# Expert bias, key and value weights and the last late tile moved across the border of two blocks

## The reference

```
x = x + attention0(LN(x), ctx, ctx)      # 64x64 products over the sequence axis, 8 heads, softmax
x = x + experts(LN(x))                   # logits x @ W_gate + b_gate, top 2 of 8 experts,
                                         # mean of relu(x @ W_e + b_e) over the two
x = x + attention1(LN(x), ctx, ctx)      # 32 query heads, 8 key/value heads of 16: k = ctx @ Wk, v = ctx @ Wv
x = x + ffn(LN(x))                       # silu(gate) * up, 1376 wide, then down
```

## Time and profile before

| | us |
|---|---|
| median of 3 runs | 899.8 (897.63 to 900.2) |
| the profiled execution | 902.44 |
| its span, first to last instruction | 900.7 |
| PE busy | 851.1 (94%) |
| DVE, ACT, POOL busy | 431.0, 347.3, 284.5 |

### The profile page before, as it was taken

The page is one execution under the profiler, slowest core; times in us unless marked ns, Lnnn a source line. Parts: engine busy times, 40 slices in busy tenths (PEclk is TensorE's granted clock), DMA queues, the critical chain, the costliest instruction groups (busy, mean ns, idle before and its releaser), DMA issues.

```text
span 900.7 us, 19749 instructions
## 1 busy us (share of the span) xinstructions
PE 851.1 (94%) x7585; PEld 693.8 (77%) x7585; DVE 431.0 (48%) x838; ACT 347.3 (39%) x567; POOL 284.5 (32%) x402
## 2 busy tenths in 40 slices
PE   5999969599999989999999899999999999999997
PEld 3788859478888867777777688878888788878885
DVE  3899955144444668888888822113122222122112
ACT  2666643133333356766666632221222122211111
POOL 3478884100000387777763231113020002002000
PEclk9999998799999999999999999999999999999999
DMA  8467675677544353555432431110030003002001
GB/s 273 136 223 248 226 254 184 234 234 265 167 165 147 120 194 90 157 164 145 135 82 54 136 108 47 37 43 1 13 116 12 1 12 106 0 23 71 1 0 48
DMA packets 55245, 105.29 MB, mean 117 GB/s; under 512 B 8210, under 2 KB 12306, under 8 KB 55026
## 3 DMA queue, kind: packets, MB, share of 16 engines
q1 hardware_dynamic: 48386, 85.02, 29.4%
q0 software_dynamic: 5120, 16.78, 5.7%
q10 hardware_dynamic: 1648, 2.23, 0.7%
HBM read 68.02 MB, written 35.98 MB: 115 GB/s over the span
## 4 chain that ended last, share of the span: by engine, by line
PE 72%; DMA 2%; POOL 2%; issue 2%; ACT 1%; DVE 1%; SPq 0%; DVEq 0%; ACTq 0%; POOLq 0%
PE c_ps L1222 9%; PE c_ps L1224 9%; PE c_ps L1223 9%; PE c_bank L1744 4%; PE c_bank L1260 3%; PE c_bank L1261 3%; PE c_bank L1266 3%; PE c_bank L1749 3%; PE c_bank L1805 3%; PE c_bank L1745 3%; PE c_bank L970 2%; PE c_ps L1780 2%; PE c_bank L971 2%; PE c_bank L976 2%; PE c_po L970 2%
## 5 line engine op out<-in xcount | busy, mean ns | idle before, releaser
L1299 DVE SCALAR_TENSOR_TENSOR d_hid<-c_ps,d_b_up,d_silu 128x512 f32<-128x512 f32 (+1 forms) x44 | 33.0, 750 | 229.3 <-PE c_ps L1224 229.3
L1222 PE MATMUL c_ps<-d_nT_hi,gate_up_hi 128*128 128x512 f32 (+1 forms) x352 | 140.7, 400 | 0.4 <-POOL gate_up_lo L1570 0.4
L1224 PE MATMUL c_ps<-d_nT_hi,gate_up_lo 128*128 128x512 f32 (+1 forms) x352 | 139.3, 396 | 0.0
L1223 PE MATMUL c_ps<-d_nT_lo,gate_up_hi 128*128 128x512 f32 (+1 forms) x352 | 139.2, 395 | 0.0
L1178 ACT ACTIVATE d_silu<-c_ps,d_b_gate 128x512 f32<-128x512 f32 (+1 forms) x44 | 30.3, 688 | 141.6 <-PE c_ps L1224 141.6
L1138 POOL TENSOR_TENSOR late_x<-late_x,d_b_down 128x512 f32<-128x512 f32 x16 | 21.8, 1390 | 187.9 <-DMA late_x<-x_after_attention 187.9
L1224 PEld LDWEIGHTS c_ps<-d_nT_hi,gate_up_lo 128*128 128x128 f32 (+1 forms) x352 | 65.7, 187 | 16.6
L1223 PEld LDWEIGHTS c_ps<-d_nT_lo,gate_up_hi 128*128 128x128 f32 (+1 forms) x352 | 65.8, 187 | 15.9
L1222 PEld LDWEIGHTS c_ps<-d_nT_hi,gate_up_hi 128*128 128x128 f32 (+1 forms) x352 | 65.7, 187 | 15.9 <-issue 0.5
L1185 ACT ACTIVATE d_hid_hi<-d_hid 128x512 fp32r<-128x512 f32 (+1 forms) x44 | 27.8, 632 | 125.7 <-DVE d_hid L1299 125.7
L989 ACT ACTIVATE b_rowsT_hi<-c_bank 128x512 fp32r<-128x512 f32 x39 | 23.3, 598 | 88.7 <-PE c_bank L959 88.7
(11 more groups left out here) (301 smaller groups left out, 1929.1 us busy)
## 6 DMA issues: line engine op xcount, KB each, us to landing
b_rows<-expert_rows SPq DMA_DIRECT2D x39, 256.0 KB, 2.7
expert_results<-b_result SPq DMA_DIRECT2D x39, 256.0 KB, 2.5
a_wstage<-L_ffn_W_e SPq DMA_DIRECT2D x16, 512.0 KB, 4.1
late_x<-x_after_attention SPq DMA_DIRECT2D x28, 256.0 KB, 3.8
c_stage<-gate_up SPq DMA_DIRECT2D x16, 344.0 KB, 3.3
out<-late_x SPq DMA_DIRECT2D x16, 256.0 KB, 2.8
x_after_attention<-late_x SPq DMA_DIRECT2D x12, 256.0 KB, 3.8
c_y_in<-x_after_attention SPq DMA_DIRECT2D x12, 256.0 KB, 2.9
```

The lines of the kernel that those rows point to most:

```text
L1222: pe.matmul(bank[0:w, :], gu_hi[:, cols], nT_hi[:, g % 2, k, :], start=k == 0, stop=False)
L1223: pe.matmul(bank[0:w, :], gu_hi[:, cols], nT_lo[:, g % 2, k, :], start=False, stop=False)
L1224: mm = pe.matmul(bank[0:w, :], gu_lo[:, cols], nT_hi[:, g % 2, k, :], start=False, stop=k == KD - 1)
```

## The change

- `load_kv_weights` no longer waits for the last query and is called in SP's step 4 instead of step 14. Wk and Wv have buffers of their own, `kv_weights`.
- `xn2` has 6 buffers (KEPT) instead of 8; the waits of `norm_x1` follow.
- In POOL's steps from 14 on, `scatter(m - 4)` comes first in the step instead of last.
- The bias is loaded in the first block, in two halves, by `load_bias`: over `probT`, `attn`, `xT`, `v` and part of `wstage`, when these are read for the last time. Half 1 goes out behind the load of ctx tile 6, half 0 behind that of ctx tile 7. DVE waits for both in front of its first bias add.
- The late tile 7 is no longer made in the first block, which still loads its ctx. PE makes it as the first thing in the second block, ACT keeps it in front of its first high part (`keep_last_kv`), SP stores it in its step 3, where it loaded the bias.
- DVE's first two bias adds no longer wait for the stores of late tiles; the first rectify still does.

```diff
--- before.py
+++ after.py
@@ -174,7 +174,7 @@
...
-    RING = 8
+    RING, KEPT = 8, 6
@@ -184,11 +184,14 @@
...
-        ctx_own, xn, xn2 = sb("ctx_own", [P, DIM]), sb("xn", [P, 2, DIM]), sb("xn2", [P, RING, DIM])
-        qT, kT, score, probT, attn, xT = (sb(n, [P, DIM]) for n in ("qT", "kT", "score", "probT", "attn", "xT"))
+        ctx_own, xn, kv_weights = sb("ctx_own", [P, DIM]), sb("xn", [P, 2, DIM]), sb("kv_weights", [P, 2, DIM])
+        qT, kT, score = (sb(n, [P, DIM]) for n in ("qT", "kT", "score"))
+        shared["bias_at"] = SBUF_END - nc.sbuf_bytes_remaining
+        probT, attn, xT = (sb(n, [P, DIM]) for n in ("probT", "attn", "xT"))
         minus_half = sb("minus_half", [P, 2, 1])
         v = sb("v", [P, 2, H0, LH + 1])
         wstage = sb("wstage", [P, 2, 1024])
+        xn2 = sb("xn2", [P, KEPT, DIM])
@@ -244,8 +247,10 @@
...
-        wk1, wv1 = (xn[:, i, :].rearrange("p (k n) -> p k n", k=KD) for i in range(2))
+        wk1, wv1 = (kv_weights[:, i, :].rearrange("p (k n) -> p k n", k=KD) for i in range(2))
         kv_stage = (qT, kT, score)
+        shared["bias"] = nc.alloc_sbuf_tensor_at("expert_bias", [P, EXPERTS * DIM], F32, offset=shared["bias_at"])
+        shared["last_kv"] = wk1, wv1, ctx_in[KV_LATE % 3].rearrange("p (k n) -> p k n", k=KD), kv_stage[(KV_LATE - 1) % 3]
@@ -317,7 +322,6 @@
             load_x(3)
             load_weights(1)
             def load_kv_weights():
-                sp.wait_ge(q_made, TILES)
                 sp.dma_start(wk1, late["Wk"].rearrange("(k p) n -> p k n", p=P)).then_inc(kvw_loaded, 16)
                 sp.dma_start(wv1, late["Wv"].rearrange("(k p) n -> p k n", p=P)).then_inc(kvw_loaded, 16)
@@ -325,6 +329,17 @@
...
+
+            def load_bias(half):
+                sp.wait_ge(o_made, TILES)
+                if half:
+                    sp.wait_ge(w_lo, TILES)
+                else:
+                    sp.wait_ge(y_made, TILES)
+                    sp.wait_ge(l_made, TILES)
+                cols = slice(half * EXPERTS * DIM // 2, (half + 1) * EXPERTS * DIM // 2)
+                rows = shared["b_e"].rearrange("e h -> (e h)")[cols].partition_broadcast(P)
+                sp.dma_start(shared["bias"][:, cols], rows).then_inc(shared["bias_loaded"][half], 16)
 
@@ -343,18 +358,24 @@
                     load_ctxT(1)
                 if tile(m - 1):
                     store_x1(m - 1)
+                if m == 4:
+                    load_kv_weights()
                 if m == TILES - 2:
-                    load_kv_weights()
                     load_ctxT(2)
                 if m == TILES - 1:
                     load_ctxT(3)
                     store_kv(0)
                     load_ctxT(4)
                     store_kv(1)
-            for i in range(2, KV_LATE):
+            for i in range(2, KV_LATE - 1):
                 if i + 3 < KV_LATE:
                     load_ctxT(i + 3)
+                if i == 3:
+                    load_bias(1)
+                if i == 4:
+                    load_bias(0)
                 store_kv(i)
+            sp.wait_ge(ctxT_loaded[(KV_LATE - 1) % 3], 16 * ((KV_LATE - 1) // 3 + 1))
             sp.wait_ge(front_zeroed, 16)
             for i in range(2):
                 sp.wait_ge(x1_stored[i], 8 * TILES)
@@ -415,9 +436,11 @@
...
-                                            in_=xn2[:, t % RING, :], in_offset=None).then_inc(scattered[t % 2], 16)
...
             for m in range(-2, TILES + 4):
+                if m >= TILES - 2 and tile(m - 4):
+                    scatter(m - 4)
                 if tile(m + 2) or tile(m - 1):
                     scale_rows(m)
                 if tile(m - 1):
@@ -426,7 +449,7 @@
                     low_part(m - 1)
...
-                if tile(m - 4):
+                if m < TILES - 2 and tile(m - 4):
                     scatter(m - 4)
@@ -454,12 +477,12 @@
...
             def norm_x1(t):
...
-                if t == RING - 1:
+                if t == KEPT - 1:
                     act.wait_ge(front_zeroed, 16)
-                if t >= RING:
-                    act.wait_ge(xt_made, t - RING + 1)
-                    act.wait_ge(scattered[t % 2], 32 * ((t - RING) // 2 + 1))
-                act.activation(xn2[:, t % RING, :], x[t % RING], ACT.Identity, scale=scales[:, (t + 1) % 2, 1, 0:1], bias=scales[:, (t + 1) % 2, 1, 1:2]).then_inc(xn2_ready, 1)
+                if t >= KEPT:
+                    act.wait_ge(xt_made, t - KEPT + 1)
+                    act.wait_ge(scattered[t % 2], 32 * ((t - KEPT) // 2 + 1))
+                act.activation(xn2[:, t % KEPT, :], x[t % RING], ACT.Identity, scale=scales[:, (t + 1) % 2, 1, 0:1], bias=scales[:, (t + 1) % 2, 1, 1:2]).then_inc(xn2_ready, 1)
@@ -516,7 +539,7 @@
...
-            for i in range(4, KV_LATE):
+            for i in range(4, KV_LATE - 1):
                 keep_kv(i)
@@ -898,19 +921,25 @@
...
-def experts(nc, c, shared, b_e, late, wq_v, proj_loaded, banks, ident, const_made):
...
     RING = 4
-    sem, sb = c.sem, Placed(nc, "b_", shared["base"] + 2 * 4 * 2 * EXPERTS * DIM).sb
-    bias = sb("bias", [P, EXPERTS * DIM])
-    rows, biased, result = sb("rows", [P, RING, DIM]), sb("biased", [P, 2, DIM]), sb("result", [P, 3, DIM])
+    sem, place = c.sem, Placed(nc, "b_", shared["base"] + 2 * 4 * 2 * EXPERTS * DIM)
+    sb = place.sb
     rowsT_hi, rowsT_lo = sb("rowsT_hi", [P, 2, DIM], F32R), sb("rowsT_lo", [P, 2, DIM], F32R)
+    biased, result = sb("biased", [P, 2, DIM]), sb("result", [P, 3, DIM])
+    place.move_to(shared["bias_at"])
+    bias = shared["bias"]
+    place.move_to(shared["bias_at"] + 4 * EXPERTS * DIM)
+    rows = sb("rows", [P, RING, DIM])
     pt, py = banks[0:2], banks[2:4]
-    bias_loaded = sem("ex_bias_loaded")
...
+    kv_made, kv_step, kv_kept = sem("ex_kv_made"), sem("ex_kv_step"), sem("ex_kv_kept")
+    wk1, wv1, ctx_rows, kv_stage = shared["last_kv"]
+    last, last_stored = KV_LATE - 1, shared["kv_stored"][(KV_LATE - 1) % 3]
@@ -944,12 +973,18 @@
...
             if b == 3:
-                sp.dma_start(bias[:, :], b_e.rearrange("e h -> (e h)").partition_broadcast(P)).then_inc(bias_loaded, 16)
+                sp.wait_ge(kv_kept, 1)
+                sp.dma_start(shared["kv"][last, :, :], kv_stage[:, 0:KV_COLS]).then_inc(last_stored, 16)
             if b >= 6:
                 store(b - 6)
...
     def tensor(pe):
+        for k in range(KD):
+            pe.matmul(kv_bank[:, 0:P], wk1[:, k, :], ctx_rows[:, k, :], start=k == 0, stop=k == KD - 1)
+        for k in range(KD):
+            mm = pe.matmul(kv_bank[:, P:2 * P], ctx_rows[:, k, :], wv1[:, k, :], start=k == 0, stop=k == KD - 1)
+        mm.then_inc(kv_made, 1)
         pe.wait_ge(const_made, 1)
@@ -983,6 +1018,17 @@
...
+        def keep_last_kv():
+            act.wait_ge(kv_made, 1)
+            act.wait_ge(last_stored, 16 * (last // 3))
+            act.activation(kv_stage[:, 0:P], kv_bank[:, 0:P], ACT.Copy).then_inc(kv_step, 1)
+            values = kv_stage[:, P:KV_COLS].rearrange("p (b j r d) -> p b j r d", b=2, j=4, r=2)
+            for r in range(2):
+                for c2 in range(2):
+                    made = kv_bank[64 * c2:64 * c2 + 64, P:2 * P].rearrange("p (j r d) -> p j r d", j=4, r=2)
+                    ins = act.activation(values[64 * r:64 * r + 64, c2, :, r, 0:HD], made[:, :, r, :], ACT.Copy)
+                    ins.then_inc(kv_kept if r and c2 else kv_step, 1)
@@ -997,6 +1043,8 @@
             act.activation(result[:, b % 3, :], biased[:, b % 2, :], ACT.Relu, scale=0.5).then_inc(result_made, 1)
 
         for b in range(BLOCKS + 2):
+            if b == 0:
+                keep_last_kv()
             if b < BLOCKS:
@@ -1014,12 +1062,10 @@
...
             if b == 0:
-                dve.wait_ge(bias_loaded, 16)
+                for loaded in shared["bias_loaded"]:
+                    dve.wait_ge(loaded, 16)
             dve.wait_ge(y_made, b + 1)
             want(dve, result_made, b - 1)
-            if b < 2:
-                for i in range(3):
-                    dve.wait_ge(shared["kv_stored"][i], 16 * ((KV_LATE + 2 - i) // 3))
             dve.tensor_tensor(biased[:, b % 2, :], py[b % 2][:, :], bias[:, bass.ds(at, DIM)], ALU.add).then_inc(biased_made, 1)
@@ -2046,6 +2092,7 @@
...
+        shared["bias_loaded"] = [kept.sem(f"bias_loaded{i}") for i in range(2)]
```

More of the change, by code:

```diff
@@ L1375, in second_attention @@
         wo_v = a["Wo"].rearrange("(k p) n -> p k n", p=P)
-        ex = experts(nc, c, shared, shared["b_e"], late, wq_v, proj_loaded, [b0, b1, b2, po], ident, const_made)
+        ex = experts(nc, c, shared, shared["b_e"], late, wq_v, proj_loaded, [b0, b1, b2, po], ident, const_made, ps[:, 0, :])
         ffn = feed_forward(nc, c, shared, ffn_args, out, Handover(
```

8 lines of the change are left out of this document (5 added, 3 removed).

## The result

The changed kernel takes **887.54 us** (886.59 to 890.85, 4 runs), against 898.71 us (896.55 to 900.2, 4 runs) for the kernel before beside it: ratio 0.9884, 95% interval 0.9848 to 0.992. Two repeats of the changed kernel gave 0.9892 (0.9858 to 0.9926) and 0.9886 (0.9865 to 0.9907). The span of the profiled execution went from 900.7 to 886.7 us, 14.0 less.

What follows compares the result with a forecast made beforehand. PE, busy 94% of the span, was taken as the bound, so only its stalls and low clock could give time. Gains of 7.8 and 5.0, 12.8 us, gave 889.6, adjusted to the median 887.0 us; 8-in-10 range 884.0 to 893.0.

Steps and rivals of the forecast that it cites:

- Early weights: SP's step 4: removes PE's 6.05 us gap, late key at 129.35 instead of 134.21; if cover fails, at most 7.1 us once.
- Scatter order: POOL's steps 14 and 15: scatter in front delays DVE's marks of tile 12 and PE's work behind by 1.2 us.
- Landing beside the bias: First block's tail: scatters land a median 5.2 us after issue, 7.0 as bound, despite 2 MB more traffic.
- my second rival: First block's tail becomes bound by DMA, scatters land with the bias: tail gain 1.8 us, total 893.0; chance 0.15.
- The second reading in the prediction: DMA completion marks land only after that engine's earlier writes across queues; at worst a scatter lands with the bias.
- The store of late tile 3: SP's queue behind the bias: lands near 151 to 152; ACT needs it for keeping tile 6 at 152.
- Level: First block's tail: late tile 3's store lands near 151 to 152, about when ACT needs it, 152.
- Head: Start of the expert block: block 3 at 182.25 instead of 187.24, gain 5.0 us, 2.0 the wait, rest clock.
- The slower side: ACT's keeping of the last tile waits for late tile 4's store behind the bias; 903 at 30 us; chance 0.03.
- 7.8 for the tail: End of the first block: POOL's drain ends at 157.0 instead of 164.8, 7.8 us earlier.
- 5.0 for the head: Start of the expert block: 5.0 us gained by block 3, 2.0 of it the bias wait, the rest clock.

Runs made afterwards that it cites:

- e3: Changed kernel, but with every scatter last in POOL's step as before: 892.2 us, ratio 0.9938 to the kernel before.
- e1: Changed kernel, but with the whole bias loaded in the expert stage behind the last late tile's store: 892.0 us, ratio 0.9943 to the kernel before.
- e7: Changed kernel, but ACT issues both bias halves early on its own queue and SP instead of POOL waits for the scatters: 891.5 us, ratio 0.9912.
- e4: Changed kernel, but with late tile 7 made at the end of the first block as before: 892.0 us, ratio 0.9951 to the kernel before.
- e12: Kernel before plus only the early weights (step 4, own buffers, six xn2 buffers): 888.7 us, ratio 0.9883 to the kernel before.
- e2: Changed kernel, but with the late key and value weights loaded at step 14 again, own buffers kept: 899.0 us, ratio 1.0016 to the kernel before.
- e11: Changed kernel, but with one bias half in the first block's tail and the other in the expert stage: 892.4 us, ratio 0.9927 to the kernel before.
- e6: Changed kernel, but SP instead of POOL waits for all scatters at the first block's end: 886.2 us, ratio 0.9861 to the kernel before.
- e13: Changed kernel, but with one bias half in the expert stage and SP instead of POOL waiting for the scatters: 888.7 us, ratio 0.9908.

## Why the prediction was right

The time was 887.54, forecast 887.0. The forecast gain was 12.8 us; the kernel gained 11.2 over the kernel before beside it, and 8.9 in each of the two repeats. By steps:

- **Early weights: right**, and at no cost, as counted. Wv landed in 7.2 us and the round stayed at 7.3. The gap and the half clock went; the late key came 2.9 us ahead of the forecast (126.42 against 129.35), 2.5 of them the earlier start of the execution, which the other times below have taken off.
- **Scatter order: right cost, wrong worth.** The delay of 1.2 us was counted, and PE's 1.92 us wait is its mark. The count of 13 was at 137.43 (137.9 forecast). But I had 15 wait for 13, as in the earlier trace rows; it didn't, since 13 went out ahead of the bias and had landed, and its last issue was at 144.45 (146.4 forecast). e3 shows what such a wait costs behind the bias: 4.6 us.
- **Landing beside the bias: under-sized.** I took the median of 5.2 us from the earlier trace rows with 7.0 as the bound; it was 8.05 here and the largest over the line is 8.4. e1, without the bias, has 4.5. The two errors, 1.95 early and 2.85 late, nearly cancel, and the tail's gain is 6.9 instead of 7.8. That the tail becomes DMA-bound and scatters land with the bias was my second rival, and it came true in part: the last scatter landed 2.9 us behind the first half. It landed 2.2 us ahead of the second, whose issue began 0.36 us after its own, too close to say that it overtook. The Trainium skill (DMA: Bandwidth & Descriptors, Queues, rings and completion order) has the engines take turns between queues packet by packet. No profile here shows a transfer that clearly gained by this: none that began behind a load of the bias passed it by more than 0.3 us, and in e7 a 256 KB load on a queue without the bias took 9.7 us. The second reading in the prediction, that a transfer issued behind the bias lands with it or behind it, is what the profiles show; whether through the order in which completions are written or only because the DMA engines were full (0.97 to 0.99), no run tells apart.
- **The store of late tile 3: under-sized.** "Level" was a wait of 4.0 us. It cost nothing that can be seen: SP left its last wait 0.4 us behind POOL, while POOL still had its drain of 2.7 us to do. That is so only because tile 7 is in the head (e4: SP 5.6 us behind).
- **Head: right.** 5.5 instead of 5.0. The clock rose about 5 us after PE began there and not 7.4. No wait for the bias. (By the prediction's own 0.23 us for a product, block 0 has 2.5 slow products and not 2.7; its end moves by less than 0.1 us.)
- **The slower side** (ACT held by the store of tile 4) did not come.

**What was wrong was the reading of the sum.** I added 7.8 for the tail and 5.0 for the head as if each part of the change had its share. e12 shows that the early weights alone give as much as the whole, within the 2 to 3 us that the intervals leave, and e2 that without them nothing is left. Given the early weights, the other three parts (scatter order, bias in the tail, tile 7 in the head) are worth this, by medians: none of them 888.7 (e12), all but the bias 892.0 (e1), all but the order 892.2 (e3), all but tile 7's move 892.0 (e4), all of them 887.5 to 889.0. The kernel before took 897.6 to 898.7 beside each. So each part taken out of the whole costs some 3 us, and the three together are worth nothing that can be seen: each mends what another costs. In profiles, the whole change has its release 1.1 us later than e12 and its head 1.6 shorter. The parts were not tried one at a time beside the early weights, so where the 3 us of e1 come from, with the bias in the head, is not shown.

Why then did the sum come out? In part by luck. The profile of before was a poor execution: 902.44 us, where the 30 runs beside e1 have a median of 897.6 and a highest of 901.57. Of these 4.8 us, 2.5 are the late start, and its bias took 10.9 us to land where that of e12 took 8.6. The steps read from it (2.0 us of wait, and the clock lost behind it) are larger than in e12, whose head has the same program; with one profile of each, which is the usual one is not shown. The forecast of 12.8 us is above the 9 to 11 that the comparisons of medians show, and it met the 887.5 partly because the base I took it off, 899.8, lay above the 897.6 to 898.7 measured since.

**What stays open**: why some executions start 2.5 us later (one profile of the kernel before is too few to tell), why the changed kernel loses 0.9 us between block 3 and the second attention, and what decides whether the clock falls behind the wait of 1.9 us.

## What to carry to other kernels

A transfer that stands directly in front of PE can be worth its whole wait and the clock behind it; moved to a round with room in its DMA engines, it cost nothing here. A bulk load moved into a stretch whose DMA engines are already 96% busy does not vanish: it reappears as longer landings of whatever is issued behind it. So look at what goes out behind the bulk load and ends the stretch, and issue that well ahead of it: 2.8 us ahead was enough for a scatter, 0.3 us was not, and another queue did not help (e7). When a change has several parts, run the likeliest one alone, and the whole without each: a right total says nothing on which part earned it.

## What the runs showed of the hardware that I had not expected

- Transfers landed behind a bulk load that was issued before them (none more than 0.3 us ahead of it), also from another engine's queue. The last scatter took 8.05 us with 1 MB ahead of it and 1 MB issued with it, 7.7 with the first alone (e11), 4.5 with neither (e1).
- A load of 256 KB on SP's queue took 9.7 us, issued 1.0 us behind the second MB on ACT's queue (e7); the same load took 2.8 us just ahead of the bias in the changed kernel.
- POOL's drain takes 2681 ns where a wait for the scatters stands before it. Without that wait it is longer (10239 ns in e6, 7853 in e7, 10771 in e13) and ends behind their landing, in e7 at 156.3, 1.4 us after the last had landed (149.38 and 5.5 us). So it seems to wait for them itself.
- After the same idle time of 1.9 us PE went on at 2.4 GHz in four profiles and fell to 1.2 in five.
